# Attention over a sparse graph: weighted sums moved into the decode, and two batches summed by ScalarE and TensorE

## The reference, cut to what matters

```
h = relu(layernorm(x)) @ W                      # x [8192, 128]
e = leaky_relu(s_src[:, None] + s_dst[None, :], 0.2)
e = where(adj > 0, e, -9e15)                    # adj [8192, 8192] int32, a share of 0.000488 is ones
out = x + softmax(e, axis=1) @ h                # s_src = h @ a[:128], s_dst = h @ a[128:]
```

## Time and profile before

| | |
|---|---|
| runs | 850.29, 851.71, 860.48 us, median 851.71 |
| profiled execution | 860.06 us, span 858.3 us |
| mean granted PE clock | 0.721 of full speed |
| DVE busy | 592.4 us, 69% |
| ACT busy | 525.0 us, 61% |
| POOL busy | 512.0 us, 60% |
| PE busy | 445.4 us, 52% |
| DMA | 299.31 MB, mean 349 GB/s |

### The profile page before, as it was taken

The page is one execution under the profiler, slowest core; times in us unless marked ns, Lnnn a source line. Parts: engine busy times, 40 slices in busy tenths (PEclk is TensorE's granted clock), DMA queues, the critical chain, the costliest instruction groups (busy, mean ns, idle before and its releaser), DMA issues.

```text
span 858.3 us, 8941 instructions
## 1 busy us (share of the span) xinstructions
PE 445.4 (52%) x1823; PEld 213.9 (25%) x1855; DVE 592.4 (69%) x3125; ACT 525.0 (61%) x371; POOL 512.0 (60%) x522
## 2 busy tenths in 40 slices
PE   4787555555555546545554545475055567533421
PEld 3652222222222222212122222132022222211221
DVE  7956577777777767566678767767177788755784
ACT  3979777666767667766387777666154877732000
POOL 3745666666656665765655666667636665665571
PEclk9888678677676777766677777777578767765555
DMA  8999999999999999989599999999659799992110
GB/s 339 424 370 419 404 408 408 408 411 407 410 409 409 408 409 405 399 315 393 217 415 411 408 409 408 408 401 409 233 210 394 277 408 409 411 402 92 25 38 11
DMA packets 40903, 299.31 MB, mean 349 GB/s; under 512 B 11052, under 2 KB 14034, under 8 KB 24464
## 3 DMA queue, kind: packets, MB, share of 16 engines
q1 hardware_dynamic: 22976, 276.83, 79.3%
q0 software_dynamic: 15328, 17.58, 6.6%
q10 hardware_dynamic: 2544, 4.33, 1.5%
HBM read 304.31 MB, written 8.65 MB: 365 GB/s over the span
## 4 chain that ended last, share of the span: by engine, by line
DVE 72%; another core or an unknown queue 11%; issue 8%; PE 5%; ACT 2%; DMA 0%; POOLq 0%; DVEq 0%; ACTq 0%
DVE x_all L821 18%; DVE rest L638 5%; DVE words L636 5%; DVE words L640 4%; PE banks L1049 3%; DVE wf L666 2%; DVE top L680 2%; DVE top_bit L662 2%; DVE cand L676 2%; DVE cand L723 1%; DVE one_hot L768 1%; DVE e L785 1%; DVE top_bit L672 1%; DVE top L727 1%
## 5 line engine op out<-in xcount | busy, mean ns | idle before, releaser
L361 POOL DMA_INDIRECT gathered<-table,index x448 | 448.7, 1002 | 295.1 <-DVE index L714 151.4
L467 ACT ACTIVATE mask_buf<-adj_buf,minus_half 128x2048 bf16<-128x2048 int32 x252 | 489.5, 1992 | 141.3 <-issue 56.5
L1049 PE MATMUL banks<-mask_buf,bit_ident 128*128 128x512 bf16 x992 | 316.6, 472 | 37.6 <-issue 24.7
L821 DVE SCALAR_TENSOR_TENSOR x_all<-gathered,weight,x_all 128x128 f32<-128x128 f32 x512 | 157.5, 348 | 16.1 <-DVE x_all L821 7.6
L1049 PEld LDWEIGHTS banks<-mask_buf,bit_ident 128*128 128x128 bf16 x1024 | 113.2, 121 | 203.4 <-issue 137.6
L1061 PE MATMUL banks<-is_wide,before 128*128 128x1 bf16 x64 | 6.9, 176 | 207.9 <-DVE is_wide L751 155.9
L1090 PE MATMUL banks<-x_all,one_hot 128*128 128x128 f32 x128 | 35.4, 368 | 74.1 <-DVE x_all L821 39.0
L481 ACT ACTIVATE prob<-e 128x16 f32<-128x16 f32 x31 | 6.5, 208 | 103.6 <-issue 72.7
L636 DVE MAX8 words<-banks 128x8 f32<-128x512 f32 x64 | 44.3, 693 | 25.4 <-PE banks L1049 18.7
L1061 PEld LDWEIGHTS banks<-is_wide,before 128*128 128x128 bf16 x64 | 4.5, 112 | 227.8 <-DVE is_wide L751 170.8
L640 DVE MAX8 words<-rest 128x8 f32<-128x512 f32 x64 | 44.5, 695 | 2.4 <-DVE rest L638 0.2
(11 more groups left out here) (162 smaller groups left out, 589.4 us busy)
## 6 DMA issues: line engine op xcount, KB each, us to landing
adj_buf<-in_adj SPq DMA_DIRECT2D x128, 2048.0 KB
gathered<-table,index POOLq DMA_INDIRECT x448
table<-gathered ACTq DMA_DIRECT2D x4, 1040.0 KB, 14.0
x_all<-in_x SPq DMA_DIRECT2D x3, 1024.0 KB, 10.8
out<-x_all SPq DMA_DIRECT2D x2, 1280.0 KB
x_all<-in_x SPq DMA_DIRECT2D x2, 512.0 KB, 5.1
out<-x_all SPq DMA_DIRECT2D x1, 1024.0 KB
w_gathered<-table,w_index POOLq DMA_INDIRECT x24
```

The lines of the kernel that those rows point to most:

```text
L361: nc.gpsimd.indirect_dma_start(g_cols[buf][:, k, :], None, table, bass.IndirectOffsetOnAxis(index[:, buf, k:k + 1], 0), bounds_check=N, oo ...
L467: nc.scalar.activation(mask_buf[:, u], adj_buf[:, u], ACT.Sign, bias=minus_half[:]).then_inc(mask_ready, 1)
L821: ins = v.scalar_tensor_tensor(at[b], g_view[par][b][:, k, 0:F], weight[:, b, k:k + 1], at[b], ALU.mult, ALU.add)
L1049: ins = mm(bank, bit_ident[:, h * PART_BITS + c], mask_buf[:, u, c * BIT_COLS:(c + 1) * BIT_COLS], start=False, stop=(h == PARTS - 1 and c ...
```

## The change

- In the ordinary iterations (batches 3 to 29) `weighted_sum` is split. Its three small steps (`weights`) run with `logits` between the two `find_words`; its eight pairs of additions (`weighted`) run in the rounds of `decode`, behind the steps of `place_wide`. Iterations 30 and 31 keep `weighted_sum` in its place.
- PE runs units 0 to 5, then `add_records`, `count_wide` and `add_sums`, then units 6 and 7.
- ACT's `wide_softmax` stands behind unit 7 instead of unit 5.
- For batches 29 and 30 DVE only makes the weights (`scaled_weights`). ACT multiplies the 16 gathered 128 x 128 blocks (`scale`), PE adds them in PSUM bank 1 by products with the identity (`add_rows`), and DVE adds the 128 x 256 result to x (`take_added`). Each block of the second batch waits until PE has read the same block of the first.

```diff
+            def scale(j):
+                act.wait_ge(weights_ready, j + 1)
+                for b in range(BATCH):
+                    for k in range(SLOTS):
+                        n = b * SLOTS + k
+                        if j > 0:
+                            act.wait_ge(row_added, (j - 1) * BATCH * SLOTS + n + 1)
+                        nc.scalar.activation(scaled[:, n], g_view[SCALED[j] % BUFS][b][:, k, 0:F], ACT.Identity,
+                                             bias=zeros[:, 0:1], scale=weight_s[:, j, b, k:k + 1]).then_inc(row_scaled, 1)
+            scale(0)
             softmax(LAST - 1)
+            scale(1)
...
+            def weighted(i):
+                for k in range(SLOTS):
+                    for b in range(BATCH):
+                        row = x_all[:, i * BATCH + b, :]
+                        ins = v.scalar_tensor_tensor(row, g_view[i % BUFS][b][:, k, 0:F], weight[:, b, k:k + 1], row,
+                                                     ALU.mult, ALU.add)
+                    if k == SLOTS - 1:
+                        ins.then_inc(out_ready, 1)
+                    yield
...
+            def take_added(j):
+                at = j * BATCH * F
+                rows = x_all[:, SCALED[j] * BATCH:(SCALED[j] + 1) * BATCH, :].rearrange("p b f -> p (b f)")
+                dve.wait_ge(row_added, (j + 1) * BATCH * SLOTS)
+                v.tensor_tensor(rows, rows, banks[:, SCALED_BANK, at:at + BATCH * F], ALU.add).then_inc(out_ready, 1)
...
-                if i >= SUM_LAG:
                     weighted_sum(i - SUM_LAG, beside=logits(i - LOGITS_LAG))
+                elif i >= SUM_LAG:
+                    alone(both_of(logits(i - LOGITS_LAG), weights(i - SUM_LAG)))
...
+                elif i >= SUM_LAG:
+                    decode(i, beside=one_by_one(place_wide(i - COUNT_LAG), weighted(i - SUM_LAG)))
...
-            weighted_sum(LAST - 3, beside=logits(LAST - 2))
+            weighted_sum(LAST - 3, beside=chained(logits(LAST - 2), scaled_weights(0)))
...
             alone(place_wide(LAST))
+            alone(scaled_weights(1))
...
-            weighted_sum(LAST - 2)
             wide_index(GROUPS - 1)
...
-            weighted_sum(LAST - 1)
+            take_added(0)
             alone(logits(LAST, 0, 1))
+            take_added(1)
             weighted_sum(LAST, 0, 1)
...
                 pack(i, 0)
-                if i >= SUMS_LAG:
-                    add_sums(i - SUMS_LAG)
-                for u in (1, 2):
+                for u in range(1, UNITS - 2):
                     pack(i, u)
                 if i >= RECORD_LAG:
                     add_records(i - RECORD_LAG)
-                pack(i, 3)
                 if i >= COUNT_LAG:
                     count_wide(i - COUNT_LAG)
-                for u in range(4, UNITS):
+                if i >= SUMS_LAG:
+                    add_sums(i - SUMS_LAG)
+                for u in range(UNITS - 2, UNITS):
                     pack(i, u)
+            def add_rows(j, lo, hi):
+                for n in range(lo, hi):
+                    k = n % SLOTS
+                    at = (j * BATCH + n // SLOTS) * F
+                    pe.wait_ge(row_scaled, j * BATCH * SLOTS + n + 1)
+                    mm(banks[:, SCALED_BANK, at:at + F], ident[:], scaled[:, n], start=(k == 0), stop=(k == SLOTS - 1)
+                       ).then_inc(row_added, 1)
```

More of the change, by code:

```diff
@@ L29 @@
 BY_TILE = (30, 31)
+SCALED = (29, 30)
+SCALED_BANK = 1
 WORD_BANKS = ((6, 7), (0, 4))
@@ L111, in gat_kernel @@
         normed, relu_t = [work[:, 0], work[:, 1]], [work[:, 2], work[:, 3]]
+        scaled = work[:, :, :, :].rearrange("p a b f -> p (a b) f")
         e_blk, p_t = normed[0], relu_t[0]
@@ L178, in gat_kernel @@
         weight = sb("weight", [P, BATCH, SLOTS], f32)
+        weight_s = sb("weight_s", [P, len(SCALED), BATCH, SLOTS], f32)
         r4 = sb("r4", [P, BATCH], f32)
@@ L231, in gat_kernel @@
             sem("w_index_ready"), sem("w_gathers"), sem("w_logits"), sem("w_exp"), sem("w_out_ready"), sem("w_stored"))
+        weights_ready, row_scaled, row_added = sem("weights_ready"), sem("row_scaled"), sem("row_added")
         unfit_ready, unfit_summed, verdict = sem("unfit_ready"), sem("unfit_summed"), sem("verdict")
@@ L497, in _ @@
                     for g in range(GROUPS - 1):
-                        if u == 5 and i == GROUP_ENDS[g] + 7:
+                        if u == UNITS - 1 and i == GROUP_ENDS[g] + 7:
                             wide_softmax(g)
@@ L795, in logits, with weights, scaled_weights, chained @@
                 yield
+            def weights(i):
+                two = i % 2
+                dve.wait_ge(exp_ready, i + 1)
+                v.tensor_reduce(max_sum[:, i % BUFS, :, 1], prob[:, two], AX.X, ALU.add)
+                yield
+                v.reciprocal(r4[:], max_sum[:, i % BUFS, :, 1])
+                yield
+                v.tensor_tensor(weight[:], prob[:, two], r4[:].unsqueeze(2).to_broadcast([P, BATCH, SLOTS]), ALU.mult)
+                yield
+            def weighted(i):
[6 more added lines that the diff above has]
+                        ins.then_inc(out_ready, 1)
+                    yield
+            def scaled_weights(j):
+                i, two = SCALED[j], SCALED[j] % 2
+                sums = max_sum[:, i % BUFS, :, 1]
+                dve.wait_ge(exp_ready, i + 1)
+                v.tensor_reduce(sums, prob[:, two], AX.X, ALU.add)
+                yield
+                v.reciprocal(r4[:], sums)
+                yield
+                v.tensor_tensor(weight_s[:, j], prob[:, two], r4[:].unsqueeze(2).to_broadcast([P, BATCH, SLOTS]), ALU.mult
+                                ).then_inc(weights_ready, 1)
+                yield
+            def take_added(j):
[3 more added lines that the diff above has]
+                v.tensor_tensor(rows, rows, banks[:, SCALED_BANK, at:at + BATCH * F], ALU.add).then_inc(out_ready, 1)
+            def chained(one, other):
+                yield from one
+                yield from other
             def alone(steps):
@@ L801, in alone, with both_of, one_by_one @@
                     settled()
+            def both_of(one, other):
+                other = iter(other)
+                for step in one:
+                    next(other, None)
+                    yield
+            def one_by_one(one, other):
+                yield from one
+                yield from other
             def weighted_sum(i, lo=0, hi=BATCH, beside=()):
@@ L912, in _ @@
                 find_words(i, 1)
-                decode(i, 1 if i in BY_TILE else 0, BATCH, beside=place_wide(i - COUNT_LAG) if i >= COUNT_LAG else ())
+                if i in BY_TILE:
+                    decode(i, 1, BATCH, beside=place_wide(i - COUNT_LAG))
+                elif i >= SUM_LAG:
+                    decode(i, beside=one_by_one(place_wide(i - COUNT_LAG), weighted(i - SUM_LAG)))
+                elif i >= COUNT_LAG:
+                    decode(i, beside=place_wide(i - COUNT_LAG))
+                else:
+                    decode(i)
                 make_records(i)
@@ L1109, in _ @@
                     add_records(i - RECORD_LAG)
-                pack(i, 3)
                 if i >= COUNT_LAG:
                     count_wide(i - COUNT_LAG)
-                for u in range(4, UNITS):
+                if i >= SUMS_LAG:
+                    add_sums(i - SUMS_LAG)
+                for u in range(UNITS - 2, UNITS):
                     pack(i, u)
+            def add_rows(j, lo, hi):
[5 more added lines that the diff above has]
+                       ).then_inc(row_added, 1)
             add_sums(LAST - 3)
+            add_rows(0, 0, SLOTS)
             add_records(LAST - 1)
+            add_rows(0, SLOTS, BATCH * SLOTS)
             count_wide(LAST)
@@ L1120, in _ @@
             mm(banks[:, 2, 8:9], ones[:], unfit_top[:], start=True, stop=True).then_inc(unfit_summed, 1)
-            for i in range(LAST - 2, BATCHES):
+            add_sums(LAST - 2)
+            add_rows(1, 0, BATCH * SLOTS)
+            for i in (LAST - 1, LAST):
                 add_sums(i)
```

## The result

The changed kernel takes 913.66 us (912.29 to 917.26) beside 856.10 us (850.29 to 866.25) for the kernel before; the ratio is 1.070, with an interval of 1.061 to 1.080. The forecast was 833 us. The profiled execution took 917.26 us, with a span of 915.5 and a granted clock of 0.71.

A forecast was written before the change was run, and what follows sets the result against it. Loads were taken to pace batches 3 to 12 and DVE, held at waits in decode, those after. Gains of 16 (DVE rounds), 1 (PE's order), 1 (batches 29 and 30) and 1 (wide gathers), 19 us, took 851.7 to 833 us; range 815 to 862.

The forecast's parts named there:

- Merged rounds on DVE: Scores and sums outside the held window: 5.9 us instead of 6.4, 0.5 us saved an iteration in batches 14 to 29.
- The held window: Held waits in decode, about 5.3 us an iteration: additions pass more work there, 0.5 us saved, bounds 0 and 1.8.
- Batches 3 to 12 are covered by the loads: Loads pace these ten iterations, so DVE's saving there counts nothing; up to 10 us more if the cover is thinner.
- PE's order: Units 6 and 7 behind add_sums: 5 us lost over 16 iterations, 6 gained at group ends; +1, bounds -24 and +6.
- The tail: Batches 29 and 30 summed through ACT and PE: 1.5 us gained, bounds -1 and +3.4, less 0.5 for a wait: 1.
- Wide gathers: Iterations with the two wide gathers: earlier index, no POOL pause, larger instructions passed; 1 us gained, bounds -10 and +10.
- Signals by time: Rival: held signals come at fixed moments, so rounds with a pair cost no more; 14 us more gained, 819 us; 17%.
- nothing on the path: Rival: loads or PE's late units pace where DVE would be faster; only 2 us gained, 850 us; 24%.
- the third rival: POOL without a pause: earlier index makes one batch's gathers meet the next's, DVE held longer; 21 us slower, 873 us; 14%.

The follow-up runs named there:

- h1: Changed kernel without the five memsets that end the scores' rounds, the step's last instruction signalling instead: 873.74 us, 1.034 of the kernel before.
- j2: Changed kernel with pairs of DVE instructions merged, 85 an iteration in place of 90: 872.10 us, 1.034 of the kernel before.
- h2: Kernel before with 16 one-column memsets added behind the first find_words of each of batches 4 to 28: 882.43 us, ratio 1.036.
- j1: Kernel before with pairs of DVE instructions merged, 80 an iteration in place of 85: 862.45 us, ratio 1.017.
- e5: Changed kernel with all eight units on PE ahead of records, flags and sums: 907.17 us, 1.056 of the kernel before.
- i1: Changed kernel without the scores' five memsets and with add_sums behind unit 7 on PE: 883.15 us, 1.033 of the kernel before.
- i2: Like i1, plus PE's old order in batches 0 to 2 and batches 29 and 30 summed on DVE: 869.76 us, 1.017 of the kernel before.
- i3: Changed kernel with 16 one-column memsets added ahead of the second find_words in batches 4 to 28: 991.02 us, 1.157 of the kernel before.
- e1: Changed kernel with add_sums moved behind unit 7 on PE: 883.08 us, 1.050 of the kernel before.
- h3: Changed kernel issuing only 2 of the last 9 wide gathers: ratio 1.046 to the kernel before, tail 51.1 us.
- e2: Kernel before with only PE's order changed, to that of the changed kernel: 846.38 us, ratio 1.0045.

## Why the forecast was wrong

- *Merged rounds on DVE: 0.5 us saved an iteration.* The time was near: DVE is busy 0.3 us less. The step that failed is the unit of account: DVE's work was priced by its duration. "The scores stand alone", 1.27 us, includes a memset in each round, and nothing was charged for the five beyond their 0.06 us each. While POOL gathers, they cost far more than that: taking the five out gave 28 to 33 us by the ratios of h1 and of the changed kernel, on different chips, and taking out five others (j2) gave the same. An ordinary iteration went up by 2.05 us where 1.0 was to be saved. h2 and j1 keep this from being a rule with a fixed price.
- *The held window: 5.3 us, from 14 us after the first gather.* I had the rows for the cost of 0.7 us an instruction and read them as a window fixed in time. It is not fixed: it opens 14.1 us after the first gather before, 13.0 in the changed kernel, 10.9 in e5. So "passes 1.4 us of work instead of 0.9" had no ground; nor do its own figures give it, since 7.5 instructions of 0.1 us are 0.75, and with half of them at 0.32 they are 1.6.
- *Batches 3 to 12 are covered by the loads.* Against a gain that held in part: j1 ran six iterations at 20.9 us and then waited for the loads, so that nine came to 22.1 us each. A DMA share of 1.01 did not mean that 22.45 us was the floor. It is no cover for a loss: 24.5 us, with the DMA share down to 0.97.
- *PE's order: 0.3 us lost in 16 iterations, bound -24.* The wait was 1.4 to 2.5 us in 21 of 27 iterations, beyond my bound of 1.5: PE's 5.4 us were inside my range, DVE's cover was 3.9 us and not 4.2 to 4.4. As a cost it was 7 us in e5 and nothing in i1. The place that I did not look at, the first batches, cost 7.7.
- *The tail: +1, bounds -1 and +3.4.* It was -8.7. L849's counterpart came 46.2 us after the last tile's first MAX8, not 34 to 38. I took the end of the wide gathers as a bound for DVE's work alone, not for PE's signals, though their issue now falls on the wait for PE.
- *Wide gathers: +1, bounds ±10.* Batch 23 gained 5.3 and batch 13 lost 1.4, inside the bounds. It may be luck: h2, with the old order and no merged rounds, has 34.3 us in batch 23 too.
- *The rivals.* Signals by time and nothing on the path did not come. POOL's pause in the ordinary iterations did not shrink, it grew from 4.5 to 6.5 us (medians). But in batches 0 and 1 it went from 2.92 us to nothing, so the third rival was right there, where I had not looked, for 7.7 of the 57 us.

Of the 62.6 us on the chip of i2, then, 36.1 are the memsets with the late words, 13.4 the start and the tail, and 13.1 stay without a cause that is shown.

## What to carry to other kernels

Where idle time on an engine is held time, count its instructions from one release to the next before summing their durations, and compare the counts of both kernels in a stretch of fixed length, over all iterations and not over three. A wait that another wait will replace is not worth its length: remove it alone, and look at what grows. When an engine issues many indirect transfers, look at the pause between two batches of them: in this kernel a pause of 3 us at the start was worth 7 us, and making the index earlier closed it. Here its run also delayed a neighbour's signal, so look for anything due at once that hangs on a signal sent while it issues.

## What the runs showed of the hardware

- While POOL issues gathers (one per 1.3 us), DVE gets through a number of instructions in 20 us that hardly depends on their length: a median of 65 before, in the changed kernel and in i3, whose work in that time is 14, 11.5 and 9.2 us. It is 72 in e1 and 74 in h2, and what sets it is not shown.
- In the held part it is one per 0.7 us: ten instructions from 282.20 to 289.17 us in the changed kernel. With 7 gathers in place of 14 the held time falls from 206 to 16 us. Memsets without input and without a signal are held as well (1.33 us in i3).
- PE is reached too: its last signal in the tail comes 13.6 us after its products, behind POOL's run, and 3.9 us after them with a shorter run in h3. In j1 a mask on ACT starts after 9.2 us of idleness during the 37 gathers; whether it was held or waited for a load is not shown.
- Gathers of two batches without a pause hold DVE longer: with 28 in a row the flags of batch 1 come at 107.02 us (e2), with a pause of 2.92 us the PE count behind them is at 93.67.
- What carries it stays open. All times here are of executions whose instructions the profiler recorded. The Trainium skill, "NOTIFIC — the notification-queue block", section "7.1 Overflow: three behaviours, one of which stalls the engine", says that the path of such records can, in one of its settings and when a ring is full, stall the engine that makes them. No run here was without the recording, so none tells whether an instruction costs a place without it.
